# A sparse graph-attention layer on one core: the feed-forward pipeline one step shorter, its edges and gathers dealt by tables

## The chip, the cores and the metric

One core of one Trainium2 chip. The metric is device microseconds for one run of the whole kernel. TensorE is called PE here, VectorE DVE, ScalarE ACT, GpSimd POOL and SyncE SP.

## What is computed

One layer of multi-head attention over a sparse graph with 2048 nodes, 256 features and 8 heads, and a feed-forward part behind it:

```
hs = layer_norm(x) ; ht = layer_norm(h_target)
q = (ht @ Wq + bq) / sqrt(32) ; k = hs @ Wk + bk ; v = hs @ Wv + bv
probs = softmax over the sources s with adj[t, s] != 0 of q[t] . k[s], per head
ht = layer_norm(ht + (probs @ v) @ Wo + bo)
out = layer_norm(x + ht + gelu(ht @ W1) @ W2)
```

The adjacency matrix has about four edges in a row (each entry is set with a chance of 0.00195).

## The kernel before

Until about 90 us the kernel projects keys and values of all nodes to a scratch in DRAM, copies h_target and x side by side to another (`tab_scratch`, a row of 2 KB for each node, after which `rows_copied` stands at 32), and turns the adjacency matrix into lists of edges. The nodes are sorted by number of edges into 16 tiles of 128 targets. Tile m has 2, 2, 2, 3, 3, 3, 4, 4, 4, 5, 5, 5, 6, 7, 8 and 16 slots (m = 0 to 15): a slot is one neighbour of each of its 128 targets.

What follows, `finish(0)`, is what the change is about. For each tile it takes these things:

- POOL issues the gathers, one indirect DMA for each slot (`fetch(m, j)`, 79 of them, of key and value rows) and one for the tile's own rows (`fetch(m, -1)`). For tiles 0 and 1 (`DIRECT = 2`) the own rows come straight from h_target, and their rows of x later through `fetch_x`.
- DVE takes the statistics of the own rows (`take_stats`), POOL raises the variance to the power -0.5 (`rsqrt_group`, L772), DVE makes the shift (`make_shift`, L1741), ACT normalises, PE transposes (`turn_own`) and projects the query.
- DVE does the edges: `weigh_keys` (a product of keys with the query, L1599, a sum over each head, L1601, then the mask, the maximum and its subtraction), ACT the exponential, and `weigh_values` (`share`, a product L1640, sums L1646 to L1661, which leave the tile's context). Tiles of more than 5 slots are cut in pieces, 12a and 12b and so on. K3 is the key work of tile 3 here, V3 its value work.
- PE transposes the context (`turn_context`) and projects it onto the residual (`project_out`), which needs ACT's copy of the context. DVE takes the statistics of that, POOL the power, DVE the shift, ACT normalises (`normalise_res`), and PE transposes (`turn_h2`).
- PE does the feed-forward part in two halves, `mlp_in` (L984), gelu on ACT, `mlp_out` (L993), and adds the transposed residual (`add_h2`, L998). DVE adds x (`add_x`, L1676), and the same chain of statistics, power, shift and normalising leads to the row scatter by POOL (`save`, L778).

All this is software-pipelined by hand in steps s = -5 to 16, in which each engine runs its own fixed order. PE's step s holds the feed-forward part of tile s, `turn_context(s + 2)` (after the first half of `mlp_in` from step 2 on, so that the second half stands behind it), `turn_h2(s + 1)` and `project_out(s + 2)`. The edges are dealt to the steps from -3 on by an estimate of their work: half of a step's pieces before `add_x`, the others between `take_stats` and `make_shift`. The gathers are dealt by a rate (`RAMP_ROWS`, `STEP_ROWS`), half of them before the step's power on POOL and half behind it. POOL is one queue in order: a power stands behind the gathers issued before it. After the last gathers POOL drains once in each step.

The time shown ends with the last scatter. A path for dense graphs (`lo = TILES`) stands behind a flag and isn't run.

## Time and profile before

| | us |
|---|---|
| median of 3 runs (333.85 to 336.05) | 333.95 |
| the profiled execution | 333.58 |
| its span, first to last instruction | 331.8 |
| PE, DVE, ACT, POOL busy | 250.6, 223.1, 157.6, 186.1 |
| first gather issued | 90.53 |
| first `mlp_in` (step 0) | 133.30 |
| last gather issued | 261.72 |
| last context ready | 297.84 |

The span and what lies around it (1.78 us) make the profiled execution's time, which is 0.37 us under the median.

### The profile page before, as it was taken

The numbers are of one execution on the slowest core, as the hardware profiler recorded it, in microseconds if no ns is written. First come the engines' busy times: TensorE is split into PE (matmuls) and PEld (weight loads), VectorE is DVE, ScalarE is ACT, GpSimd is POOL, SyncE is SP. The second block draws the span as 40 slices with busy tenths as digits, with TensorE's granted clock in tenths as the row PEclk, the third lists the DMA queues.
The fourth block names the chain that finished last, engine by engine and source line by source line (L and its number), as shares of the span: only waits on it lengthen the run. The fifth ranks groups of instructions, "written<-read, shape, count | busy, mean of one in ns | idle before, by whom it ended". The sixth has DMA issues, their size and how long they took to land.

```text
span 331.8 us, 4310 instructions
## 1 busy us (share of the span) xinstructions
PE 250.6 (76%) x1383; PEld 195.3 (59%) x1383; DVE 223.1 (67%) x623; ACT 157.6 (47%) x282; POOL 186.1 (56%) x204
## 2 busy tenths in 40 slices
PE   6599895650216745979999899899895796949990
PEld 6344331210112524967999799789784695939980
DVE  3489879798825437367897698688885589780111
ACT  1656999610014323465767567746752244303220
POOL 8776522390077765725777888887878603111211
PEclk9789979875555565979999999999999599787996
DMA  6999999999546645424346564454565700000000
GB/s 159 401 396 418 418 391 328 355 303 333 207 131 185 191 132 169 143 64 126 113 147 171 159 174 144 132 166 147 161 174 168 155 28 16 18 0 16 16 17 24
DMA packets 23490, 58.04 MB, mean 175 GB/s; under 512 B 4051, under 2 KB 12517, under 8 KB 21414
## 3 DMA queue, kind: packets, MB, share of 16 engines
q0 software_dynamic: 8400, 27.01, 28.1%
q1 hardware_dynamic: 14228, 29.91, 24.7%
q10 hardware_dynamic: 834, 0.79, 1.1%
q8 instruction: 13, 0.21, 0.2%
q14 instruction: 15, 0.12, 0.1%
HBM read 51.40 MB, written 10.49 MB: 187 GB/s over the span
## 4 chain that ended last, share of the span: by engine, by line
PE 28%; POOL 26%; issue 17%; DVE 15%; ACT 9%; DMA 2%; another core or an unknown queue 1%; POOLq 0%; ACTq 0%; DVEq 0%
POOL arena L746 12%; PE score L984 8%; PE bank L993 7%; PE bank L854 4%; POOL rstd_late L772 4%; POOL tab L736 3%; DVE arena L1599 2%; DVE arena L1640 2%; DVE logits L1601 2%; POOL out_dram L778 2%; ACT arena L1174 2%; PE bank L962 2%; DVE arena L1646 2%; ACT query L1182 2%; ACT arena L1165 1%
## 5 line engine op out<-in xcount | busy, mean ns | idle before, releaser
L746 POOL DMA_INDIRECT arena<-kv_scratch,places x79 | 82.7, 1047 | 22.5 <-issue 22.5
L984 PE MATMUL score<-h_t,w_sb 128*128 128x128 f32 x512 | 66.3, 286 | 2.0 <-ACT h_t L1299 2.0
L984 PEld LDWEIGHTS score<-h_t,w_sb 128*128 128x128 f32 x512 | 64.9, 203 | 3.4 <-ACT h_t L1299 2.6
L993 PE MATMUL bank<-w_sb,gelu_t 128*128 128x256 f32 x256 | 62.1, 395 | 5.4 <-issue 4.8
L993 PEld LDWEIGHTS bank<-w_sb,gelu_t 128*128 128x128 f32 x256 | 50.3, 200 | 13.5 <-issue 5.4
L1245 ACT ACTIVATE gelu_t<-score 128x512 f32<-128x512 f32 x32 | 19.1, 597 | 68.2 <-PE score L984 51.2
L772 POOL TENSOR_TENSOR rstd_late<-var_late,minus_half 128x2 f32<-128x2 f32 (+2 forms) x22 | 22.2, 1009 | 34.6 <-DVE var_late L1711 24.3
L778 POOL DMA_INDIRECT out_dram<-y_out,places x16 | 17.1, 1071 | 34.0 <-ACT y_out L1291 30.8
L854 PE MATMUL bank<-tab,arena 128*128 128x512 f32 x64 | 32.9, 668 | 0.8 <-DVE arena L1423 0.4
L1599 DVE TENSOR_TENSOR arena<-arena,query 128x1024 f32<-128x1024 f32 (+3 forms) x22 | 24.6, 1116 | 7.9 <-ACT query L1276 6.5
L1676 DVE SCALAR_TENSOR_TENSOR y_sum<-bank,place_value,tab 128x256 f32<-128x256 f32 x16 | 7.7, 480 | 30.4 <-PE bank L998 29.2
L1640 DVE TENSOR_TENSOR arena<-arena,logits 128x1024 f32<-128x1024 f32 (+3 forms) x22 | 24.6, 1117 | 0.6
L1601 DVE TENSOR_REDUCE logits<-arena 128x32 f32<-128x1024 f32 (+3 forms) x22 | 24.4, 1111 | 0.8
L657 POOL TENSOR_TENSOR v_total<-v_total,arena 128x256 f32<-128x256 f32 x15 | 11.9, 796 | 22.4 <-DVE arena L1423 20.9
L854 PEld LDWEIGHTS bank<-tab,arena 128*128 128x128 f32 x64 | 13.4, 220 | 17.2 <-issue 16.3
L1252 ACT ACTIVATE tab<-tab,shift_late,rstd_late 128x256 f32<-128x256 f32 x16 | 9.4, 599 | 29.1 <-DVE shift_late L1741 29.1
L947 PE MATMUL score<-wq_sb,own_t 128*128 128x256 f32 x64 | 20.0, 443 | 0.0
L962 PE MATMUL bank<-wo_sb,ctx_t 128*128 128x256 f32 x64 | 19.0, 425 | 0.0
L1299 ACT ACTIVATE h_t<-bank,ln_col 128x128 f32<-128x128 f32 x32 | 12.9, 455 | 12.8 <-PE bank L971 10.0
L1646 DVE TENSOR_TENSOR arena<-arena 128x256 f32<-128x256 f32 (+1 forms) x32 | 17.1, 535 | 1.1
L736 POOL DMA_INDIRECT tab<-tab_scratch,places x14 | 15.2, 1088 | 4.0 <-issue 3.7
L1267 ACT ACTIVATE own_t<-score,ln_col 128x128 f32<-128x128 f32 x32 | 12.9, 456 | 8.1 <-PE score L937 7.9
(153 smaller groups left out, 447.2 us busy)
## 6 DMA issues: line engine op xcount, KB each, us to landing
arena<-in_adj_dram SPq DMA_DIRECT2D x6, 1024.0 KB, 11.8
w_sb<-in_adj_dram SPq DMA_DIRECT2D x6, 1024.0 KB, 12.9
kv_scratch<-arena SPq DMA_DIRECT2D x8, 512.0 KB, 9.7
tab<-in_x_dram SPq DMA_DIRECT2D x4, 512.0 KB, 11.0
own_t<-in_adj_dram SPq DMA_DIRECT2D x2, 1024.0 KB, 14.8
gelu_t<-in_adj_dram SPq DMA_DIRECT2D x2, 1024.0 KB, 11.4
tab_scratch<-in_L_gnn_h_target_dram SPq DMA_DIRECT2D x1, 2048.0 KB, 12.0
tab_scratch<-in_x_dram SPq DMA_DIRECT2D x1, 2048.0 KB, 16.5
```

The lines of the kernel that those rows point to most:

```text
L736: pool.indirect_dma_start(tab[:, m % TR, :], None, tab_dram[:, :], at).then_inc(own_gathered[m % OWN_RING], 16)
L746: pool.indirect_dma_start(kv_ring[:, ring_at[m] + j, :], None, kv_dram[:, :], at).then_inc(gathered[m][piece], 16)
L772: pool.tensor_tensor(rstd_late[:, a:b], var_late[:, a:b], minus_half[:, 0:b - a], ALU.pow).then_inc(rstd_late_ready, 1)
L778: pool.indirect_dma_start(out[:, :], bass.IndirectOffsetOnAxis(ap=places[:, at:at + 1], axis=0), y_out[:, n % YR, :], None).then_inc(y_sav ...
L854: mm = pe.matmul(proj_ps[i % 2], h_t[:, c % 2, k, i * P:(i + 1) * P], wkv[:, k, :], start=(k == 0), stop=(k == DK - 1))
L962: mm = pe.matmul(attn_ps[:, 0:D], ctx_t[:, n % 2, k, :], wo_sb[:, k, :], start=False, stop=(k == DK - 1), skip_group_check=True)
L984: mm = pe.matmul(hid_ps[(2 * n + half) % 3][:, f % 4 * P:(f % 4 + 1) * P], w1_sb[:, k, f * P:(f + 1) * P], h2_t[:, n % 2, k, :], start=(k ...
L993: pe.matmul(ff_ps[:, 0:D], gelu_t[:, n % 2, f, :], w2_sb[:, f, :], start=(f == 0), stop=False, skip_group_check=True)
L1599: dve.tensor_tensor(keys, keys, asked, ALU.mult).then_inc(score_step, 1)
L1601: dve.tensor_reduce(logits[:, r, a:b, :], keys.rearrange("p j (h d) -> p j h d", h=H), AX.X, ALU.add).then_inc(score_step, 1)
L1640: dve.tensor_tensor(by_head, by_head, part, ALU.mult).then_inc(weigh_step, 1)
L1646: dve.tensor_tensor(values[:, 0:half, :], values[:, 0:half, :], values[:, left - half:left, :], ALU.add).then_inc(weigh_step, 1)
```

## The change

- Steps -5 to -1 are gone for the sparse path. In their place every engine has a lead-in written out instruction by instruction: five tiles' own rows, K0 to K2, V0, V1, the first `project_out` and `turn_h2`, with a power for each row of statistics of its own (six, where steps -5 to -1 had five).
- In a step, `project_out(s + 1)` takes the place of `project_out(s + 2)`, right behind the first half of `mlp_in(s)`, and `turn_context(s + 2)` goes to the end of the step, behind `add_h2(s)`.
- `STEP_EDGES` says by name which pieces DVE does in each step behind `add_x`, between `take_stats` and `make_shift`, and behind `make_shift`. `OWN_STEP` says in which step a tile's own rows are taken, `OWN_AT` and `ROWS_BY` when gathers are issued.
- All own rows come from the copied table with their x: the two `fetch_x` go, and the first gather waits for `rows_copied`.
- ACT's order follows, and the two kinds of identity products (in `project_out` and `add_h2`) are written as transposes.

```diff
-    EDGES_LEAD = 3
-    RAMP = 0.35
-    DIRECT = 2
-    CONTEXT_LATE = 1
-    RAMP_ROWS, STEP_ROWS = 3, 6.5
+    OWN_STEP = [-5, -4, -3, -2, -1, 0, 1, 1, 2, 3, 4, 4, 5, 6, 7, 8]
+    OWN_AT = [0, 0, 3, 4, 10, 13, 18, 20, 29, 31, 39]
+    ROWS_BY = [(6, 12), (12, 16), (20, 23), (27, 30), (33, 37), (39, 45), (46, 50), (54, 58), (62, 67), (67, 71), (72, 76), (78, 81), ...
+    STEP_EDGES = [
+        ("V2 K3", "", "K4"),
+        ("", "V3", "K5 V4"),
+        ("V5", "", "K6"),
+        ("V6", "K7", "V7"),
+        ("", "K8", "V8"),
+        ("K9", "", "K10 V9"),
+        ("", "", "K11 K12a"),
+        ("V10", "K12b", "K13a V11"),
+        ("V12a", "V12b", "K13b"),
+        ("V13a", "K14a", "K14b"),
+        ("V13b", "K15a", "V14a"),
+        ("K15b", "", "V14b"),
+        ("K15c", "K15d", "V15a V15b"),
+        ("", "V15c", "V15d"),
...
+        lead_fetches = [(0, -1), (0, 0), (0, 1), (1, -1), (ROOT, 0), (2, -1), (1, 0), (ROOT, 1), (1, 1), (3, -1), (ROOT, 2),
+                        (2, 0), (2, 1), (4, -1), (ROOT, 3), (3, 0), (ROOT, "res"), (3, 1), (ROOT, 4), (3, 2)]
...
                 for k in range(DK):
                     pe.matmul(attn_ps[:, k * P:(k + 1) * P], own_t[:, own_of(n) % OWN_RING, k, :], ident[:, :], start=False,
-                              stop=False, skip_group_check=True)
+                              stop=False, is_transpose=True, skip_group_check=True)
...
@@ PE, finish @@
+                if lo == 0:
+                    for o in range(2):
+                        turn_own(o)
+                        project_query(o)
+                    turn_tally()
+                    turn_own(2)
+                    turn_context(0)
+                    project_out(0)
+                    project_query(2)
+                    turn_own(3)
+                    turn_h2(0)
+                    project_query(3)
...
+                for s in range(lo, hi):
+                    own_now = [own_of(lo + m) for m in own_work[s - lo - 1]]
+                    first = lo == 0 and s == 0
+                    mlp_in(s, 0)
+                    if s + 1 < hi and not first:
+                        project_out(s + 1)
+                    if own_now:
+                        turn_own(own_now[0])
+                    if first:
+                        turn_context(1)
+                    mlp_in(s, 1)
+                    if own_now:
+                        project_query(own_now[0])
+                    if first:
+                        project_out(1)
+                    mlp_out(s, 0)
+                    if len(own_now) > 1:
+                        turn_own(own_now[1])
+                    if s + 1 < hi:
+                        turn_h2(s + 1)
+                    mlp_out(s, 1)
+                    add_h2(s)
+                    if len(own_now) > 1:
+                        project_query(own_now[1])
+                    if lo == 0 and s + 2 < hi:
                         turn_context(s + 2)
@@ DVE @@
+            def lead():
+                def own_stats(m):
+                    take_stats(("lead", m), [m], None, None)
+
+                own_stats(0)
+                make_shift(("lead", 0))
+                own_stats(1)
+                make_shift(("lead", 1))
+                own_stats(2)
+                weigh_keys(0, 0, SLOTS[ORDER[0]])
+                make_shift(("lead", 2))
+                sum_tally()
+                weigh_values(0, 0, SLOTS[ORDER[0]])
+                own_stats(3)
+                weigh_keys(1, 0, SLOTS[ORDER[1]])
+                make_shift(("lead", 3))
+                take_stats(("lead", "res"), [], 0, None)
+                set_flag()
+                make_shift(("lead", "res"))
+                weigh_values(1, 0, SLOTS[ORDER[1]])
+                own_stats(4)
+                weigh_keys(2, 0, SLOTS[ORDER[2]])
+                make_shift(("lead", 4))
...
-                    early = 0 if s == lo - 1 else len(edges_now) if s < lo else len(edges_now) // 2
+                    first, second, rest = parts_of(s) if lo == 0 else ([], [], [])
                     key = (lo, s - lo)
-                    weigh_edges(edges_now[:early])
                     if s > lo:
                         add_x(s - 1)
+                    weigh_edges(first)
                     if key in group_at:
                         take_stats(key, [own_of(lo + m) for m in own_work[s - lo]],
                                    s + 1 if lo <= s + 1 < hi else None, s - 1 if s > lo else None)
-                    if s >= lo:
-                        weigh_edges(edges_now[early:])
+                    weigh_edges(second)
                     if key in group_at:
                         make_shift(key)
-                    if s < lo:
-                        weigh_edges(edges_now[early:])
+                    weigh_edges(rest)
```

## Rows read from the trace of the kernel before

**Rows 1.** The table by stage: busy of each engine, granted clock, DMA share, GB/s.

```profile
89.00:133.30 44.30, 22.15 (x71) 14.33 (x72) 21.13 (x75) 12.35 (x31) 30.79 (x34) 0.56 0.51 151
133.30:262.70 129.40, 117.04 (x764) 105.46 (x763) 99.37 (x230) 78.12 (x148) 97.26 (x89) 0.97 0.51 147
262.70:297.90 35.20, 27.48 (x171) 24.94 (x169) 27.62 (x56) 11.11 (x21) 7.35 (x6) 0.89 0.12 27
297.90:331.80 33.90, 25.37 (x155) 23.47 (x155) 4.71 (x18) 7.84 (x16) 5.99 (x7) 0.85 0.06 18
```

**Rows 2.** POOL's groups from 89 to 263 us: busy, mean ns, idle before.

```profile
L746 POOL DMA_INDIRECT arena<-kv_scratch,places x79 | 82.7, 1047 | 22.5 <-issue 22.5
L772 POOL TENSOR_TENSOR rstd_late<-var_late,minus_half 128x3 f32<-128x3 f32 (+2 forms) x16 | 16.4, 1025 | 11.1 <-DVE var_late L1711 9.7 <-issue 1.0
L778 POOL DMA_INDIRECT out_dram<-y_out,places x9 | 9.6, 1068 | 5.6 <-ACT y_out L1291 3.2 <-issue 2.4
```

**Rows 3.** The timeline of the last three steps and the end.

```profile
296.23 1.15 DVE L1646 TENSOR_TENSOR arena<-arena 128x512 f32<-128x512 f32 x2
297.41 0.42 DVE L1661 TENSOR_TENSOR context<-arena 128x256 f32<-128x256 f32 x1
298.37 3.62 PE L984 MATMUL score<-h_t,w_sb 128*128 128x128 f32 x16
301.79 3.96 PE L993 MATMUL bank<-w_sb,gelu_t 128*128 128x256 f32 x16
...
323.76 0.48 DVE L1676 SCALAR_TENSOR_TENSOR y_sum<-bank,place_value,tab 128x256 f32<-128x256 f32 x1 [5.98 <-PE bank L998]
```

**Rows 4.** The timeline of the lead-in, 90 to 134 us.

```profile
90.53 1.25 POOL L730 DMA_INDIRECT tab<-in_L_gnn_h_target_dram,places  x1 [14.99 <-DVE place_value L1568]
98.99 1.92 PE L947 MATMUL score<-wq_sb,own_t 128*128 128x256 f32 x4
110.26 0.95 POOL L736 DMA_INDIRECT tab<-tab_scratch,places  x1 [0.30 <-issue]
113.83 0.43 DVE L1697 BATCH_NORM_STATS2 stats_own<-tab 128x6 f32<-128x256 f32 x1 [2.81 <-DMA tab<-tab_scratch,places]
120.33 0.43 DVE L1697 BATCH_NORM_STATS2 stats_own<-tab 128x6 f32<-128x256 f32 x1 [4.66 <-DMA tab<-tab_scratch,places]
133.30 1.95 PE L984 MATMUL score<-h_t,w_sb 128*128 128x128 f32 x16
```

**Rows 5.** One step on PE in the steady part, from the timeline.

```profile
169.87 1.95 PE L984 MATMUL score<-h_t,w_sb 128*128 128x128 f32 x16
173.99 1.03 PE L947 MATMUL score<-wq_sb,own_t 128*128 128x256 f32 x4
174.85 3.62 PE L993 MATMUL bank<-w_sb,gelu_t 128*128 128x256 f32 x16
178.52 0.61 PE L998 MATMUL bank<-ident,h_t 128*128 128x128 f32 x4
180.39 1.95 PE L984 MATMUL score<-h_t,w_sb 128*128 128x128 f32 x16
```

**Rows 6.** Edge work on DVE by shape, from 93 to 298 us.

```profile
L1599 DVE TENSOR_TENSOR arena<-arena,query 128x1024 f32<-128x1024 f32 x10 | 12.2, 1224 | 0.0
L1646 DVE TENSOR_TENSOR arena<-arena 128x512 f32<-128x512 f32 x13 | 9.0, 692 | 0.4
```

**Rows 7.** Places of the timeline where something was late without a cause in the program.

```profile
162.88 1.22 DVE L1599 TENSOR_TENSOR arena<-arena,query 128x1024 f32<-128x1024 f32 x1
163.01 1.83 POOL L772 TENSOR_TENSOR rstd_late<-var_late,minus_half 128x3 f32<-128x3 f32 x1
174.58 0.90 POOL L772 TENSOR_TENSOR rstd_late<-var_late,minus_half 128x3 f32<-128x3 f32 x1
258.33 0.60 ACT L1245 ACTIVATE gelu_t<-score 128x512 f32<-128x512 f32 x1 [6.57 <-remote]
266.32 0.48 DVE L1676 SCALAR_TENSOR_TENSOR y_sum<-bank,place_value,tab 128x256 f32<-128x256 f32 x1 [4.53 <-PE bank L998]
```

More of the change, by code:

```diff
@@ L477, in graph_attention @@
[L477 to L491 removed]
+        LEAD_KEYS, LEAD_VALUES = 3, 2
@@ new lines, in stretch_of, with parts_of @@
+        def stretch_of(name):
+            m = int(name[1:].rstrip("abcd"))
+            letter = name[1:].lstrip("0123456789")
+            a, b = pieces_of(m)["abcd".index(letter) if letter else 0]
+            return KEYS if name[0] == "K" else VALUES, m, a, b
+        def parts_of(step):
+            return [[stretch_of(name) for name in part.split()] for part in STEP_EDGES[step]]
+        edge_work = {step: [w for part in parts_of(step) for w in part] for step in range(TILES + 1)}
+        for stage, first in ((KEYS, LEAD_KEYS), (VALUES, LEAD_VALUES)):
+            assert [w[1:] for some in edge_work.values() for w in some if w[0] == stage] == [
+                (m, a, b) for m in range(first, TILES) for a, b in pieces_of(m)]
@@ L508, in graph_attention @@
                     add_group(("own", o), [("own", o)])
-            for step in range(-LEAD, TILES + 1):
+            else:
+                for some in (0, 1, 2, 3, "res", 4):
+                    add_group(("lead", some), [("res", 0) if some == "res" else ("own", some)])
+            for step in range(0 if lo == 0 else -LEAD, TILES + 1):
                 some = [("own", own_of(lo + m)) for m in own_work[step]]
@@ L1003, in finish @@
                 hi = lo + TILES
-                for s in range(lo - LEAD, hi):
-                    own_now = [own_of(lo + m) for m in own_work[s - lo - 1]] if s > lo - LEAD else []
-                    if lo == 0 and s == 1 - EDGES_LEAD:
-                        turn_tally()
-                    if s >= lo:
-                        mlp_in(s, 0)
+                if lo == 0:
+                    for o in range(2):
[9 more added lines that the diff above has]
+                    project_query(3)
+                else:
+                    for m in range(LEAD - 1):
+                        turn_own(own_of(lo + m))
+                        project_query(own_of(lo + m))
+                    project_out(lo)
+                    turn_h2(lo)
@@ L1016, in finish @@
-                    for o in own_now[:1]:
-                        project_query(o)
-                    if s >= lo:
-                        mlp_out(s, 0)
-                    if lo == 0 and s <= CONTEXT_LATE and lo <= s + 2 < hi:
-                        turn_context(s + 2)
-                    if s >= lo:
-                        mlp_out(s, 1)
-                    if lo <= s + 1 < hi:
-                        turn_h2(s + 1)
-                    if s >= lo:
-                        add_h2(s)
@@ L1239, in exponential, with exponentials @@
                 act.activation(part, part, ACT.Exp).then_inc(exp_done, 1)
+            def exponentials(some):
+                for stage, m, _, b in some:
+                    if stage == KEYS and b == SLOTS[ORDER[m]]:
+                        exponential(m)
             def gelu(n, half):
```

184 lines of the change are left out of this document (79 added, 105 removed).

## Prediction

> **What bounds the kernel now.** I read the table by stage first, because the shares of the whole span hide that three engines take turns. Between 133.3 us (the first `mlp_in`) and 262.7 (the last gather issued) PE is busy 117.0 of 129.4 us, DVE 99.4 and POOL 97.3 [rows 1]. The second view, POOL's groups, shows that POOL is nearly full there all the same: each of the 79 gathers has 22.5/79 = 0.28 us of "issue" in front, so one costs 1.05 + 0.28 = 1.33 us, a save (9.6 + 2.4)/9 = 1.33, a power 1.03 and about 0.2 behind it [rows 2]. After 262.7 no gather is left, and the work that ends last is DVE's: pieces b to d of K15, then V14 and V15, until the last context at 297.41 + 0.42 = 297.8 [rows 3]. Then PE does the second half of tile 13's feed-forward part and all of tiles 14 and 15 in its fixed order, `add_x` starts at 323.76, and the span ends at 331.8. The kernel from 90.5 us on is therefore three stretches in a row, and I forecast each: the lead-in (90.5 to 133.3), steps 0 to 13 (133.3 to 297.8, 164.5 us), the tail (34.0 us).
>
> **The lead-in.** Both versions do K0 to K2, V0, V1 and the first `project_out` before step 0. In the old one a step's statistics wait for own rows far ahead: DVE stands 2.81 us for tile 5's row, gathered from 110.26 and used at 113.83, and 4.66 us for the next at 120.33, and the first residual's chain stands behind them [rows 4]. The written-out order asks only for tiles 0 to 4. I follow it:
> - Gather of row 0 at 90.5 as before. The new wait for `rows_copied` costs nothing if the copy has landed; POOL went past the same wait at tile 2's row before. A row of 2 KB takes 113.83 - 110.26 = 3.6 us from issue to use [rows 4], about 0.4 more than the 1 KB rows that go.
> - Query 0 is projected at 98.99 as before, queries 1 and 2 follow in about 4.6 and 7 us, because `turn_own` waits until the query before is copied and PE runs at its lower level there (mean granted clock 0.56 from 89 to 133.3 [rows 1]; four products take 1.92 us against 1.03 later [rows 4, 5]). `project_out(0)` ends near 110.5, its statistics, power and shift near 112. POOL stands idle about 2.6 us at this power and 1.3 at the next: a new loss, as gathers are queued behind.
> - `project_query(2)`, `turn_own(3)`, normalising, `turn_h2(0)` and `project_query(3)` follow one another on PE: the first `mlp_in` starts near 118.3. That is 15.0 us before 133.3.
> - DVE ends K2 at 116.7 and waits for tile 2's exponential (behind ACT's long list) until 119.6, 13.7 us before its old start of step 0. POOL ends its 14 lead gathers at 116.3. It had issued about 19 by then, so it is some 6 us behind its old place.
>
> **Steps 0 to 13.** The pieces in them are the same as before (V2 and K3 up to V15), and so are the statistics. DVE's busy time for them is 99.4 + 27.6 = 127.0 us in 286 instructions [rows 1]; an instruction starts a little behind its predecessor's end (0.03 us between the first two rows of [rows 3]; I take 0.05 as the mean, an estimate, since small ones in chains wait longer), so they occupy about 143 us, and 164.5 - 143 = 21.5 were waits. Part of the waits had no cause in the program: ACT stood 6.57 us before the gelu at 258.33, and DVE 4.53 for PE behind it [rows 7].
> Added is a loop within one step. `project_out(s + 1)` now ends about 3.0 us into PE's step (half an `mlp_in` 1.8, bias, two transposes and four products 1.2), and `turn_h2(s + 1)` stands about 8.1 us into it [rows 5] (half an `mlp_in` 1.8 us, a query 1.0, `mlp_out` 3.5, by the distances between starts). Between them lie DVE's statistics (0.9), the pieces in the middle column, the wait for POOL, a power (0.9), shift (0.2) and ACT (0.6). In front there are the pieces of the first column. A 4-slot piece costs 2 x 1.22 us for keys and 1.22 + 0.69 + 0.43 for values, with some 0.6 to 0.9 more for a tile's end [rows 6]. Steps 3 and 7 hold over 6 us in the first two columns: PE waits some 2 and 4.5 us there, elsewhere 0 to 3. PE can afford it: a step with a query took 180.39 - 169.87 = 10.5 us [rows 5], and 14 steps of at most that are 147, under DVE's 143 plus waits. The transposes halve four instructions' worth in `add_h2` and `project_out`, 0.4 us a step, on PE alone; nothing of it reaches the end but 1 us in the tail.
> POOL: step 0 has 12 gathers, six before its power (116.3 + 8 = 124.5), but the power waits for `project_out(1)` until about 128.5: 4 us idle. From there the hand walk goes: DVE starts `add_x` of steps 4, 8 and 12 at 169, 219 and 261 us. DVE waits at `make_shift` in steps 0, 2, 3, 5 and 6 because gathers stand before the power (1 to 3 us each), 3.6 in step 0 for PE, about 1 us for an exponential in four steps. The last gather is issued near 260, 81 x 1.33 + 11 x 1.33 + 12 x 1.2 = 137 us of work and 7 of idle behind 116.3. It lands 3.6 later, in time for K15d at 264.6. V15d ends at 284.0. That is 143 of work and 21.4 of waits from 119.6, so the same length as before: 164.4. It holds no unexplained standstill, and the old stretch had about 5 us of them on DVE's path. I add 3 for such: 287.0.
>
> **A rule on the power.** A power on three values took 0.90 us at 174.58, but 1.83 at 163.01, where DVE's product of two arrays in SBUF ran from 162.88 for 1.22 us [rows 7]. The Trainium skill (SBUF — State Buffer, Who interferes with whom) says that a `tensor_tensor` with both inputs in SBUF and a GpSimd operation that reads SBUF exclude each other for a whole instruction. The trace agrees at these two rows. By the rule alone the new order would be a little better: it has a product beside the power in 9 steps of 14 (those with a middle column), the old one in all 14, and 5 x 0.93 us less would give 309. I keep the mean of 1.03, because in the five others DVE has nothing to do but wait for the power.
>
> **The tail.** Now `turn_context(15)` ends step 13 and doesn't stand before its second half. Gone from behind the last context are half an `mlp_in` and an `mlp_out`, 3.62 + 3.96 with overlap 7.2 us at that clock, `turn_h2` and `add_h2`, 0.7, and 1 us of slow clock and transposes [rows 3, 5]. 34.0 - 9.0 = 25.0 us: turn and copy 0.4, step 14 with `project_out(15)` 8.7, step 15 7.9, then 331.8 - 323.76 = 8.0. This holds if PE is through step 13 when V15d ends; by the walk it is just behind (283.8).
>
> **Sum.** 287.0 + 25.0 = 312.0 us of span, plus 333.58 - 331.8 = 1.8: 313.8, or 314, against 333.58 for the profiled execution and 333.95 for the median (which I leave as the same). It is 13.7 by the lead, 9.0 by the tail and -3 by the allowance, since the walk's 164.4 replaces 164.5 that held standstills already.
>
> **Rivals.**
> 1. POOL gives the lead's gain back. POOL is 6 us behind at 116 and idle 8 us by 128.5; any further idle puts the last gather past 270, and K15d with V15 takes 20 us behind it. For: the old last gather was at 262 and the new one is at 260 in my walk, without slack. Then DVE ends near 297 as before and only the tail is won: 333.6 - 9.0 = 324.6.
> 2. The tables fill DVE's waits. Each piece is placed by name, and DVE may wait 9 us where it waited 21. Against: the powers stand behind gathers in order. 119.6 + 143 + 9 + 25.0 + 1.8 = 298.4.
> 3. Slower: the loop of one step. PE, DVE and POOL meet twice in a step (at the power, at `turn_h2`), with one step of slack less. If each step has one gather more before its power (1.33) and a power held by a product (0.93 more [rows 7]), it costs 2.26 us x 14 = 31.6 on the walk: 345. The point where it decides is (333.6 - 313.8)/14 = 1.4 us a step. Against: PE had 12 us to spare in the long stretch [rows 1].
> 4. The change shifts nothing that counts: the lead's gain lost in the steps as in 1, and PE not through step 13 at V15, so that the tail's gain goes too: 333.
>
> **How the numbers follow.** Forecast 0.50 (306 to 321), rival 1 0.22, rival 2 0.17, rival 3 0.06, rival 4 0.05. Within 1% (3.3 us) is about what a measurement of this kernel tells from no change. The range goes from 300 to 327, which leaves out the best part of rival 2, and rivals 3 and 4. Faster by over 1%: 0.89; within 1%: 0.06; slower: 0.05.
>
> **What would show it.** In the changed kernel: the first `mlp_in` near 118 and DVE's V2 near 120; the last gather near 260; the last context near 287; no `mlp_in` of tile 13 behind it; 25 us from there to the end; PE idle before `turn_h2` by waits for ACT in several steps, above all step 7. I am wrong if PE's first `mlp_in` is later than 125, if POOL idles over 15 us before its last gather, or if DVE's stretch from V2 to V15 is over 175 or under 158 us.

## The result and the profile after

The changed kernel took 317.38 us (median of 4 runs, 317.19 to 318.49), the kernel before 333.9 on the same occasion (332.99 to 336.05): ratio 0.950, 95% interval 0.946 to 0.954, faster. I had said 314 and 300 to 327. The profiled execution took 318.49, with a span of 316.8. Executions over 1.5% above the fastest of the same kernel are left out of every ratio here; three of four were such in experiments 2 and 5, which have no ratio, and the traces of experiments 2, 5 and 8 are of such executions.

The table by stage of the changed kernel, cut where mine were cut: start of step 0, last gather issued, last context. The columns are those of [rows 1].

```profile
89.00:115.10 26.10, 13.79 (x44) 8.30 (x44) 14.89 (x55) 8.47 (x21) 17.26 (x20) 0.56 0.46 131
115.10:266.40 151.30, 128.68 (x824) 114.54 (x824) 113.51 (x271) 94.12 (x171) 115.90 (x103) 0.97 0.52 148
266.40:291.80 25.40, 19.11 (x112) 16.75 (x111) 20.00 (x38) 9.40 (x17) 5.47 (x5) 0.89 0.14 36
291.80:316.80 25.00, 17.98 (x118) 16.32 (x116) 4.71 (x17) 5.59 (x11) 5.97 (x7) 0.91 0.07 24
```

The first row took 44.3 us and now takes 26.1. The last took 33.9 and takes 25.0. What lies between is 176.7 us (151.3 + 25.4) in place of 164.6. So some 27 us were won at the two ends and 12 are longer in the middle (part of that is DVE work that has only moved there from the lead-in, as said below). The middle is what the experiments are about.

The lead-in, from the timeline (it answers to [rows 4]):

```profile
90.50 1.25 POOL L739 DMA_INDIRECT tab<-tab_scratch,places  x1 [15.00 <-DVE place_value L1611]
98.94 1.92 PE L946 MATMUL score<-wq_sb,own_t 128*128 128x256 f32 x4
...
109.53 1.91 PE L946 MATMUL score<-wq_sb,own_t 128*128 128x256 f32 x4
114.17 1.03 PE L946 MATMUL score<-wq_sb,own_t 128*128 128x256 f32 x4
115.12 2.05 PE L983 MATMUL score<-h_t,w_sb 128*128 128x128 f32 x16
```

The first own row and the first query stand where they stood. The last query of the lead takes 1.03 us where the others take 1.91: the granted clock is 0.50 from 108 to 112 us and 1.00 from 112.2 on, so PE is at the higher of its two levels (2.4 GHz) again before step 0.

POOL's groups from 89 to 268 us, against [rows 2]:

```profile
L749 POOL DMA_INDIRECT arena<-kv_scratch,places x79 | 88.0, 1114 | 22.2 <-issue 22.2
L769 POOL TENSOR_TENSOR rstd_late<-var_late,minus_half 128x1 f32<-128x1 f32 (+3 forms) x18 | 17.8, 991 | 13.2 <-DVE var_late L1752 12.0 <-issue 0.9
...
L775 POOL DMA_INDIRECT out_dram<-y_out,places x10 | 12.0, 1197 | 3.0 <-issue 3.0
```

The same 79 gathers take 88.0 us in place of 82.7. The issue gap in front of each is unchanged.

The end, from the timeline, against [rows 3]:

```profile
291.36 0.42 DVE L1704 TENSOR_TENSOR context<-arena 128x256 f32<-128x256 f32 x1
...
293.70 1.95 PE L983 MATMUL score<-h_t,w_sb 128*128 128x128 f32 x16
...
309.81 0.48 DVE L1717 SCALAR_TENSOR_TENSOR y_sum<-bank,place_value,tab 128x256 f32<-128x256 f32 x1 [4.17 <-PE bank L997]
```

From the last context's end (291.78) to `add_x` of tile 15 are 18.0 us; they were 25.9.

Three things in this trace were not in my working. One is a stall on POOL, between its last save before step 13 and the power of step 13:

```profile
278.06 1.11 POOL L775 DMA_INDIRECT out_dram<-y_out,places  x1 [7.29 <-ACT y_out L1306]
288.10 0.72 POOL L769 TENSOR_TENSOR rstd_late<-var_late,minus_half 128x2 f32<-128x2 f32 x1 [8.93 <-issue]
```

POOL waits for nothing that the profile shows, for 8.93 us. The program has a `pool.drain()` at this place, in both kernels. In the old one the same 8.93 us ended at 273.31 and DVE had edge work meanwhile; here DVE and PE wait for the power.

The second follows from it. My tail asked that PE be through step 13 when the last context is ready (291.78). It wasn't:

```profile
289.66 0.69 PE L970 MATMUL bank<-ident,h 128*128 128x128 f32 x2 [3.08 <-ACT h L1298]
290.14 3.29 PE L992 MATMUL bank<-w_sb,gelu_t 128*128 128x256 f32 x8
...
293.49 0.38 PE L928 MATMUL bank<-ident,context 128*128 128x128 f32 x2
```

PE had stood 3.08 us for the `h` of tile 14, and came to `turn_context(15)` 1.7 us after the context.

The third is that PE's results come late although its own rows run on:

```profile
166.96 1.95 PE L983 MATMUL score<-h_t,w_sb 128*128 128x128 f32 x16
...
172.00 0.60 ACT L1260 ACTIVATE gelu_t<-score 128x512 f32<-128x512 f32 x1 [2.62 <-remote]
173.45 0.43 DVE L1746 BATCH_NORM_STATS2 stats_late<-bank 128x6 f32<-128x256 f32 x1 [4.88 <-remote]
```

`mlp_in` should be through at 168.9, and gelu starts at 172.00. "Remote" is the profile's word for a wait whose releaser it can't name; the old trace had such places too [rows 7]. I call them standstills. The name says no more than that: no run here shows what PE, or the record of it, does in them. From 100 to 300 us, ACT and DVE together spent 18.8 us in such waits here, and 21.2 in the old trace. The waits of the two engines overlap.

### The profile page after: what moved, and what is told of

It is laid out like the page before. It is cut to its first block, busy times and chain, and to the rows that moved or that the text cites. A ratio compares the mean times of both kernels' runs of the same rounds, so it can differ in the third digit from the quotient of the medians.

```text
span 316.8 us, 4181 instructions
## 1 busy us (share of the span) xinstructions
PE 236.4 (75%) x1316; PEld 183.1 (58%) x1319; DVE 223.7 (71%) x625; ACT 165.7 (52%) x286; POOL 189.4 (60%) x203
## 3 DMA queue, kind: packets, MB, share of 16 engines
q1 hardware_dynamic: 14228, 29.91, 25.9%
## 4 chain that ended last, share of the span: by engine, by line
PE 32%; POOL 21%; issue 13%; DVE 10%; ACT 10%; DMA 8%; another core or an unknown queue 4%; SPq 1%; POOLq 0%; ACTq 0%; DVEq 0%
POOL arena L749 12%; PE bank L992 8%; PE score L983 7%; DMA tab_scratch<-in_x_dram 5%; PE bank L853 4%; POOL rstd_late L769 3%; PE bank L961 3%; PE score L946 3%; POOL tab L739 3%; POOL out_dram L775 2%; ACT arena L1188 2%; ACT query L1196 2%; DMA arena<-kv_scratch,places 2%; ACT arena L1179 2%
## 5 line engine op out<-in xcount | busy, mean ns | idle before, releaser
L749 POOL DMA_INDIRECT arena<-kv_scratch,places x79 | 88.0, 1114 | 22.2 <-issue 22.2
L992 PE MATMUL bank<-w_sb,gelu_t 128*128 128x256 f32 x256 | 66.5, 408 | 0.0
L983 PE MATMUL score<-h_t,w_sb 128*128 128x128 f32 x512 | 62.5, 276 | 0.0
L983 PEld LDWEIGHTS score<-h_t,w_sb 128*128 128x128 f32 x512 | 60.3, 193 | 0.6 <-ACT h_t L1314 0.3
L992 PEld LDWEIGHTS bank<-w_sb,gelu_t 128*128 128x128 f32 x256 | 51.5, 208 | 7.1
L769 POOL TENSOR_TENSOR rstd_late<-var_late,minus_half 128x1 f32<-128x1 f32 (+3 forms) x23 | 21.1, 918 | 31.7 <-DVE var_late L1752 21.6
L1260 ACT ACTIVATE gelu_t<-score 128x512 f32<-128x512 f32 x32 | 19.1, 597 | 30.7 <-PE score L983 22.9
L853 PE MATMUL bank<-tab,arena 128*128 128x512 f32 x64 | 31.1, 636 | 1.3 <-DVE arena L1466 1.1
L739 POOL DMA_INDIRECT tab<-tab_scratch,places x16 | 17.3, 1079 | 19.3 <-DVE place_value L1611 15.0
L970 PE MATMUL bank<-ident,h 128*128 128x128 f32 x32 | 7.8, 331 | 25.0 <-ACT h L1298 21.3
L970 PEld LDWEIGHTS bank<-ident,h 128*128 128x128 f32 x32 | 3.7, 153 | 30.0 <-ACT h L1298 25.2
L1746 DVE BATCH_NORM_STATS2 stats_late<-bank 128x6 f32<-128x256 f32 x16 | 6.9, 429 | 18.3 <-PE bank L961 10.1
L946 PE MATMUL score<-wq_sb,own_t 128*128 128x256 f32 x64 | 19.1, 427 | 0.0
L1282 ACT ACTIVATE own_t<-score,ln_col 128x128 f32<-128x128 f32 x32 | 12.9, 454 | 11.4 <-PE score L936 5.3
L1314 ACT ACTIVATE h_t<-bank,ln_col 128x128 f32<-128x128 f32 x32 | 12.9, 453 | 10.2 <-PE bank L970 9.5
## 6 DMA issues: line engine op xcount, KB each, us to landing
arena<-in_adj_dram SPq DMA_DIRECT2D x6, 1024.0 KB, 12.2
tab<-in_x_dram SPq DMA_DIRECT2D x4, 512.0 KB, 11.6
tab_scratch<-in_L_gnn_h_target_dram SPq DMA_DIRECT2D x1, 2048.0 KB, 12.1
```

The costliest lines, as they stand in the source:

```text
L739: pool.indirect_dma_start(tab[:, m % TR, :], None, tab_dram[:, :], at).then_inc(own_gathered[m % OWN_RING], 16)
L749: pool.indirect_dma_start(kv_ring[:, ring_at[m] + j, :], None, kv_dram[:, :], at).then_inc(gathered[m][piece], 16)
L769: pool.tensor_tensor(rstd_late[:, a:b], var_late[:, a:b], minus_half[:, 0:b - a], ALU.pow).then_inc(rstd_late_ready, 1)
L853: mm = pe.matmul(proj_ps[i % 2], h_t[:, c % 2, k, i * P:(i + 1) * P], wkv[:, k, :], start=(k == 0), stop=(k == DK - 1))
L946: mm = pe.matmul(own_ps[:, D:KV], own_t[:, o % OWN_RING, k, :], wq_sb[:, k, :], start=False, stop=(k == DK - 1))
L983: mm = pe.matmul(hid_ps[(2 * n + half) % 3][:, f % 4 * P:(f % 4 + 1) * P], w1_sb[:, k, f * P:(f + 1) * P], h2_t[:, n % 2, k, :], start=(k ...
```

## The experiments

All are edits of the changed kernel. They ran on four occasions, and the kernel before ran beside them each time: 331.7 us on the first (four kernels), 335.3 on the second (four), 328.8 on the third (three), 328.9 on the fourth (one). Differences are taken within an occasion wherever I can. In the record the first and the fourth occasion have the same chip number (13); the second has 6 and the third 11. Before experiment 12 I compared traces with the changed kernel's first one, which has standstills; where experiment 12's trace, which has none, changes a reading, it is said there.

**1. `turn_context` back in mid-step (the tail).** From step 2 it stands again before the second half of `mlp_in`, not at the end of PE's step.

```
+                    if lo == 0 and s > 1 and s + 2 < hi:
+                        turn_context(s + 2)
...
-                    if lo == 0 and s + 2 < hi:
+                    if lo == 0 and s <= 1:
                         turn_context(s + 2)
```

> The changed kernel with turn_context(s + 2) put back in front of the second half of mlp_in(s), from step 2 on (ACT's copy of it again behind the second gelu). Tail theory: 7 us of feed-forward work of tile 13 stand behind the last context again, so the last context comes at the same 291.8 us and the tail is 32 to 34 us instead of 25.0: 325 us. Rival (PE is not through step 13 anyway when the last context is ready, so the order hardly matters): within 2 us of 317.4.

322.75 us (319.04 to 323.41), ratio 0.973 (0.965 to 0.981). PE's waits from 116 to 300 us:

```profile
PE bank L970 <- ACT h L1300: 19.1, 11, 3.9
PE bank L928 <- DVE context L1708: 10.7, 1, 10.7
```

PE stands 10.7 us at `turn_context` for the last context, with half an `mlp_in` and an `mlp_out` of tile 13 behind it. The last context ends at 289.6 and the span at 320.7: a tail of 31.1 us in place of 25.0. So 6.1 of the 9 us that the tail won are this one move.

**2. PE's old order, two tiles ahead (the loop in one step).** `project_out(1)` is done in the lead, and `project_out(s + 2)` at the end of PE's step. `turn_context(s + 2)` is back in mid-step as in experiment 1.

```
+                    turn_context(1)
+                    project_out(1)
...
-                    if s + 1 < hi and not first:
-                        project_out(s + 1)
...
+                    if s + 2 < hi:
+                        project_out(s + 2)
```

> The changed kernel with PE's old order: project_out(s + 2) at the end of step s, turn_context(s + 2) in the middle of it, and project_out(1) in the lead-in; tables and lead-in stay otherwise. Theory of the loop in one step: PE stood 25 us in front of turn_h2, DVE 15 us in front of make_shift; with a step of slack PE's waits there fall under 10 us and the stretch from V2 to V15 shrinks from 175 us by 5 to 10; the tail is 8 us longer and the lead-in 2: about 320 us. Rival (POOL's gathers in order set the stretch, whatever the order on PE): it stays at 173 to 177 us, and the whole is 327 us.

326.33 us (318.09 to 329.08, the 318.09 without a trace); last context at 292.7, tail 32. PE's wait for ACT's `h` at `turn_h2` is 21.0 us in 10 places; it is 20.0 in 9 in the changed kernel from 116 to 300 us. With a whole step of slack given back, PE waits as long. The stretch from V2's first row (117.40) to the last context is 175.3 us, to the tenth what it is in the changed kernel's first profile (with 12.2 us of waits without a releaser for 18.8 there). So the loop within one step does not set its length, as far as one trace tells. I read it so that `h` is late because the power is late: DVE waits 15.8 us for powers here (12.1 there).

**3. Eight gathers fewer (POOL's queue).**

```
+        LEFT_OUT = [(m, SLOTS[ORDER[m]] - 1) for m in range(6, 14)]
...
-                else:
+                elif (m, j) not in LEFT_OUT:
                     if (m, j) == (0, 0):
...
```

> The changed kernel with the last gather of each of the tiles 6 to 13 left out (8 of 79; the slot's old content is used, so those edges are wrong), DVE's work unchanged. It is 8 x 1.35 = 11 us less for POOL. If POOL's queue sets the stretch from V2 to V15, it shrinks by 7 to 11 us: 307 to 310 us. If DVE's own work and its meetings with PE set it: under 3 us: 315 to 317. There are 103 indirect DMAs in it in place of 111: by the count theory of the 8.93 us that standstill is gone, by the drain theory it is there.

306.26 us (305.03 to 307.68), ratio 0.926 (0.919 to 0.932).

```profile
L750 POOL DMA_INDIRECT arena<-kv_scratch,places x71 | 76.6, 1079 | 19.8 <-issue 19.8
```

POOL is spared 11.4 + 2.4 = 13.8 us and the last context ends at 278.0, 13.8 before its place in the changed kernel's first profile. About 1.7 of that was there already at the first context, and this profile has fewer standstills (3.6 us in place of 18.8), so 13.8 is more than the gathers' worth. Against experiment 12, which has no standstill, it is much less: the stretch from V2 to the last context is 164.0 us here and 167.2 there, 3.2 shorter for 15.6 us less of gathers on POOL. (This profile has one standstill, of 3.6 us, so without it at most 6.8.) With eight gathers fewer POOL is no longer full: from 116 us to its last gather it waits 11.6 us for DVE and ACT. DVE had the same work and followed POOL's queue only in part. The stall before the power was still there, 8.27 us.

**4. Nothing ahead of the power in the queue, from step 2 to step 11.** The gathers that the table puts in front of a step's power go behind it.

```
-    ROWS_BY = [(6, 12), (12, 16), (20, 23), (27, 30), (33, 37), ...
+    ROWS_BY = [(6, 12), (12, 16), (16, 23), (23, 30), (30, 37), ...
```

> The changed kernel with no gather in front of the power in steps 2 to 11 (all of a step's gathers behind it). Theory of the loop in one step (DVE's 15 us and PE's 25 us of waits are the gathers in front of powers): these waits fall by half and the whole by 3 to 6 us: 312 to 314. Queue theory: POOL itself stands idle until each step's statistics are there, 1 to 3 us a step more, the last gather comes later than 268 by 5 to 15 us, and the whole takes 320 to 330.

329.38 us (328.37 to 332.7), ratio 0.984 (0.981 to 0.986), 9 us slower than experiment 7 on the same occasion. Its profile has 31.8 us of waits without a releaser and that of experiment 7 has 20.2, so how much of the 9 is the queue's is not shown.

```profile
L769 POOL TENSOR_TENSOR rstd_late<-var_late,minus_half 128x1 f32<-128x1 f32 (+3 forms) x23 | 22.5, 979 | 45.0 <-DVE var_late L1752 34.5
```

POOL stands 34.5 us for the variances (21.6 in the changed kernel) with its gathers behind the waiting power. The last gather is issued at 281.06 in place of 266.42. Where gathers stand in front of the power, the power is late; where they stand behind it, the gathers are.

**5. The powers of the steps on DVE** (two Newton rounds there, none of these powers on POOL).

```
-            return key[0] != "own"
+            return key[0] in ("lead", TILES)
...
```

> The changed kernel with the power of each of the steps 0 to 16 worked out on DVE (a first guess from the exponent and two rounds of Newton, 7 small instructions, 1.3 us) in place of POOL's. POOL has 17 x 1.2 = 20 us less to do and no power stands behind its gathers; DVE doesn't wait for POOL at make_shift (15 us), but has 14 x 1.3 = 18 us more of its own. Queue theory (POOL's queue in order sets the stretch from V2 to V15): the last gather comes 10 to 14 us earlier, the stretch shrinks by 5 to 10, and the tail by 0 to 2: 308 to 313 us. Rival (DVE's own work is the bound as much as POOL): 317 or more.

355.14 us (349.16 to 355.96). DVE's busy time goes from 223.7 to 242.8, so the added work is 19 us and the loss nearer 35. The profile has 60 us of waits without a releaser on ACT and DVE; the first `add_x` is already 7.6 us late. How much of the loss is theirs can't be read off. This experiment decides nothing about the queue: the 19 us on DVE are one cause, and the rest is open.

**6. The port that DVE and POOL share: one-input sums in place of the edge products.**

```
-                dve.tensor_tensor(keys, keys, asked, ALU.mult).then_inc(score_step, 1)
+                dve.tensor_reduce(spare[:, a:b, :], keys.rearrange("p j (h d) -> p j h d", h=H), AX.X,
+                                  ALU.add).then_inc(score_step, 1)
```

(and the same for the product with the weights.)

> The changed kernel with the two products of the edges (keys with the query, values with the weights: two arrays from SBUF) replaced by sums over the same elements (one array from SBUF) into a spare tile, so that scores and contexts are wrong and DVE's time is nearly the same (1.11 us each in both forms). In the changed kernel gathers that start within a product take 1.9 to 2.3 us in place of 0.95, and all 79 take 88.0 us. Lock theory (a gather's issue on POOL waits until DVE's product of two SBUF arrays is over): the long ones go, the 79 take under 80 us, the last gather is issued 6 to 9 us earlier, and with it the whole ends near 309. Rival (gathers are long because of their own data or DMA): they stay at 1.11 us in the mean, and the whole at 317.

322.73 us (322.42 to 326.66), ratio 0.968 (0.960 to 0.975): so the time didn't come down to the 309 that I expected, but POOL's durations did what they should:

```profile
L750 POOL DMA_INDIRECT arena<-kv_scratch,places x79 | 77.5, 981 | 22.2 <-issue 22.2
...
L770 POOL TENSOR_TENSOR rstd_late<-var_late,minus_half 128x1 f32<-128x1 f32 (+3 forms) x23 | 17.0, 738 | 43.6 <-DVE var_late L1754 34.5
```

Gathers are 10.5 us cheaper and powers 4.1, and POOL spends it waiting. On ACT and DVE there are 35.6 us of waits without a releaser. No run has this kernel without them; experiments 10 and 11 make the same comparison with half the bytes, and there they are absent.

**7. PE's products without `is_transpose`.**

```
-                              stop=False, is_transpose=True, skip_group_check=True)
+                              stop=False, skip_group_check=True)
```

> The changed kernel with the identity products of project_out and add_h2 as plain matrix products again (twice as many instructions). Prediction: 0.4 us a step on PE, of which only about 1 us in the tail counts: 318 to 319 us, tail 26 us. Rival (PE is in the loop of each step, so each step pays): 14 x 0.4 = 6 us, 323 us.

320.35 us (319.43 to 325.92), ratio 0.957 (0.954 to 0.960). The last context is at 291.6 (291.8 in the changed kernel), the tail 26.0 in place of 25.0: by one trace of each the cheaper form is worth about 1 us, in the tail.

**8. No drain.**

```
-                        pool.drain()
```

> The changed kernel without POOL's drains behind the last gather. In both kernels POOL stood 8.93 us in front of one power after the gathers were over. If a drain causes it, it goes, DVE doesn't wait 2.1 us at make_shift(13) nor PE 3.1 us at turn_h2(14), and the kernel takes 314 to 315.5 us. Rival (it comes with the 107th indirect DMA, since 107 were issued before it in both kernels): the 8.93 us stay where they are, 317 us.

317.35 us (314.97 to 321.04), ratio 0.957 (0.947 to 0.967).

```profile
283.47 1.62 POOL L769 TENSOR_TENSOR rstd_late<-var_late,minus_half 128x2 f32<-128x2 f32 x1 [4.86 <-DVE var_late L1752]
...
308.57 1.03 POOL L775 DMA_INDIRECT out_dram<-y_out,places  x1 [1.11 <-ACT y_out L1306]
```

The power no longer waits: it starts at 283.47, and the last scatter is out at 309.6 in place of 314.0. But the span ends at 319.3, 9.7 us behind that scatter, where the changed kernel ends 2.8 behind its own and every other profile here 2.7 to 4.0. In this execution the time that was removed stands at the end. Two of the four runs took 315; they have no trace, so whether they escaped it is not known. As a whole the interval (0.947 to 0.967) holds the changed kernel's 0.950: no gain is shown.

**9. The drain in a gap.** It goes in front of the save of step 12, where POOL had 7.29 us of idle time.

```
+                    if lo == 0 and step == FIRST_DRAIN:
+                        pool.drain()
                     if s > lo:
                         save(s - 1)
...
```

> Whole computation kept. POOL's first drain is moved from behind the save of step 12 (where it stood 8.93 us until 288.10 and DVE and PE waited for the power behind it) to in front of that save, where POOL had 7.29 us of idle time (270.77 to 278.06). Theory (the 8.93 us are the time of a drain after many indirect DMAs, and must be paid once, wherever it stands): the drain lasts from about 270.8 to 279.7, the save is 1.6 us later, which nobody waits for; the power of step 13 comes near 283.5 as in the kernel without the drain, last context near 289.0 (before 291.8), and the end, without the late cost that the kernel without the drain had in some runs, near 314.5 (313.5 to 315.5). Rival (the drain waits for the last gathers or saves to finish in some other way, and stands just as long at any later place, or makes the following drains long): a second stall of several us before a later power, 317 to 318. Rival (the save held back by 2 us makes ACT or POOL late in step 13): 316 to 317.

303.62 us (301.96 to 305.4, 6 runs), ratio 0.924 (0.920 to 0.928): 11 us better than the 314.5 I expected, and I expected only 4 of it from this edit.

```profile
267.86 1.23 POOL L776 DMA_INDIRECT out_dram<-y_out,places  x1 [9.53 <-issue]
270.79 1.61 POOL L770 TENSOR_TENSOR rstd_late<-var_late,minus_half 128x2 f32<-128x2 f32 x1 [1.70 <-DVE var_late L1755]
```

The stall is 9.53 us, in front of a save that nobody waits for, and the power behind it waits 1.70 us for its variance alone. But step 11 had ended at 253.48 already, 12 us early, with the program unchanged up to there. The trace has not one wait without a releaser. Whether that is the edit's doing is what run 12 asks.

**10. Half the bytes per gather.**

```
-                    pool.indirect_dma_start(kv_ring[:, ring_at[m] + j, :], None, kv_dram[:, :], at).then_inc(
+                    pool.indirect_dma_start(kv_ring[:, ring_at[m] + j, 0:D], None, kv_half[:, :], at).then_inc(
...
```

> All 79 edge gathers of the steps and the lead bring 1 KB of each of 128 rows in place of 2 KB (from a view of half rows), and the value products use the keys' half, so scores and contexts are other numbers; the count of gathers, their places in POOL's order and every instruction of the engines stay. What it is to tell: what the standstills are in which PE's results come 2 to 5 us late and the trace names no releaser (in the changed kernel 8.1 us of DVE's waits, 10.7 of ACT's between 116 and 300 us). Theory T (DMA traffic: the standstills fall in stretches in which the 16 DMA engines are 70% busy or more with gathered rows): the DMA share falls to about 0.4 there, waits without a releaser fall under 3 us on each of the two engines, POOL's own rate stays (1.1 us a gather and 0.28), and the time falls by what of the standstills lay on POOL's or DVE's path: 310 to 315. Rival P (they come from POOL's issuing of descriptors back to back, whatever the bytes): waits without a releaser stay at 6 us or more on DVE or ACT, 316 to 318.5. Rival N (gathers themselves get faster with fewer bytes): the mean of a gather falls under 1.0 us, 305 to 310.

310.56 us (309.02 to 313.33), ratio 0.943 (0.937 to 0.948). No standstill, but run 9, with all the bytes, had none either, so it says nothing of their cause. It does say that bytes don't set a gather's price on POOL (with 2 KB a row it is 1136 ns in experiment 12):

```profile
L750 POOL DMA_INDIRECT arena<-kv_scratch,places x79 | 91.4, 1157 | 22.2 <-issue 22.2
```

**11. Half the bytes and one-input sums.** The edits of experiments 6 and 10 together.

> As the kernel with half the bytes per gather, and besides DVE's two edge products of every piece are replaced by sums with one input (as in the earlier run, which had gathers of 981 ns on the mean but 322.7 us in all, more than the changed kernel); scores and contexts are other numbers. Theory T (gathers closer together in time filled the DMA engines and made more standstills, which ate what POOL had saved): with half the bytes the standstills are gone, gathers keep about 0.98 us, and the time comes out where the rule on the shared port alone put it, 306 to 311, below the kernel with half the bytes by 3 us or more. Rival P (standstills come with POOL's rate of issue, not with bytes): 319 to 324 again. Rival M (the sums themselves are slower for DVE or order the work worse): no standstills, but 316 to 321, with DVE's or ACT's named waits longer.

299.33 us (299.19 to 299.69), ratio 0.910 (0.906 to 0.914).

```profile
L751 POOL DMA_INDIRECT arena<-kv_scratch,places x79 | 77.8, 985 | 22.2 <-issue 22.2
```

11.2 us below run 10, whose only difference is the form of DVE's products. DVE is busy as long in both (222.5 and 223.3 us), so it isn't the sums that are cheaper. In the traces the stretch from V2 to the last context is 158.1 us against 168.4, 10.2 shorter, for 13.6 us less of gathers and 1.5 of powers. POOL has room again: from 116 us to its last gather it waits 9.5 us for DVE and ACT.

**12. The changed kernel again, unaltered.**

> The changed kernel itself, unaltered, on another occasion. The last batch ran where the kernel before took 328.75 us, and none of its three profiles had a standstill without a releaser; the one with the earlier drain took 303.6 us, far under my 314.5. Theory V (the standstills belong to the chip or the occasion, not to the program: without them the changed kernel takes about 308, and the earlier drain is worth 4 to 5 us of it): if no standstill shows in this profile, 306 to 310, with the step ends of the kernel with the earlier drain up to step 11 (first at 125.4, the twelfth at 253.5, within 3 us), then the 8.9 us before the power of step 13. If standstills show (8 us or more on ACT or DVE), 315 to 319 again and the twelfth step end past 262. Rival W (placing the drain earlier changed the whole run, by code alignment or otherwise): no standstill here and yet 314 or more, or standstills here on an occasion where the kernel before takes 329 or less.

308.14 us (305.6 to 310.2, 6 runs) against 328.9: ratio 0.934 (0.930 to 0.937), with no wait without a releaser in the profile, as theory V had it. This occasion's chip number is that of experiments 1, 2, 3 and 8, which had standstills, so they are no fixed property of one chip. The ends of steps 3, 4 and 11 (`add_x`), first in the changed kernel's first profile, then in this one:

```profile
167.11 0.48 DVE L1717 SCALAR_TENSOR_TENSOR y_sum<-bank,place_value,tab 128x256 f32<-128x256 f32 x1
180.77 0.48 DVE L1717 SCALAR_TENSOR_TENSOR y_sum<-bank,place_value,tab 128x256 f32<-128x256 f32 x1
...
265.91 0.48 DVE L1717 SCALAR_TENSOR_TENSOR y_sum<-bank,place_value,tab 128x256 f32<-128x256 f32 x1 [0.30 <-PE bank L997]
```

```profile
163.35 0.48 DVE L1717 SCALAR_TENSOR_TENSOR y_sum<-bank,place_value,tab 128x256 f32<-128x256 f32 x1
174.57 0.48 DVE L1717 SCALAR_TENSOR_TENSOR y_sum<-bank,place_value,tab 128x256 f32<-128x256 f32 x1
...
256.58 0.48 DVE L1717 SCALAR_TENSOR_TENSOR y_sum<-bank,place_value,tab 128x256 f32<-128x256 f32 x1 [0.30 <-PE bank L997]
```

V2 starts 1.17 us apart in the two (116.48 and 115.31). At the end of step 3 they are 3.8 apart, of step 4 6.2, then level to step 7, 8.0 at step 8 and 9.3 at steps 10 and 11. Each growth sits where the first profile has a standstill (gelu or statistics at 134.06, 161.32, 172.00, 227.00 and 249.20) and nowhere else. The standstills cost the first run 9.3 - 1.2 = 8.1 us.

This trace also shows the middle without them. The stretch from V2's first row to the last context, and POOL's waits for the input of a power, from 116 us to its last gather at 257.08:

```profile
115.31:282.52 167.21, 144.60 (x924) 128.95 (x924) 132.88 (x304) 102.97 (x184) 119.74 (x108) 0.97 0.49 139
```

```profile
POOL rstd_late L769 <- DVE var_late L1752: 1.5, 2, 1.2
```

With another 0.3 us before an own row, POOL waits 1.8 us for another engine in 141 us, against 8.0 in the first profile. It is full: what puts the last gather where it is are its own entries.

Against run 12, the earlier drain of run 9 is worth 308.14 - 303.62 = 4.5 us. By the traces, from `add_x` of step 11 to the end of the span, it is 51.5 us there and 46.7 in run 9, so 4.8: 3.1 of them before the last context and 1.7 in the tail (23.9 in place of 25.6). The two kernels ran on different occasions and chips, but the kernel before took the same beside both (328.75 and 328.9). The intervals of the two ratios (0.930 to 0.937, 0.920 to 0.928) don't touch. This version beats both kernels.

## Why the prediction was right

- **The sum.** 313.8 against 318.49 for the profiled execution and 317.38 for the median. Two errors of size are in it, which cancel in part: the lead 3.1 us too late, and the steps 7.9 too short. So the three stretches and their gains were right, and the closeness of the sum is in part luck. By one sign that I had named I was wrong: the stretch from V2 to V15 was 175.3 us, over my 175.
- **The lead-in** was won as said, and more: step 0's `mlp_in` at 115.12 (I had 118.3), V2 at 116.48 (119.6). `project_out(0)` ended at 109.5 (I had 110.5) and its shift at 111.2 (112). The other 2 us came behind it: I went on with the lower level's durations, and the granted clock was 1.00 from 112.2; that this makes all of the rest is not shown. The own row took 3.69 us from issue to use, as said.
- **Steps 0 to 13.** I had 167.4 from V2 to the last context, 3 of them an allowance for standstills; measured 175.3. Run 12 has 167.2 (115.31 to 282.52), so the total was right where no standstill fell, but by luck. I wrote that the pieces in the steps are the same as before, V2 and K3 up to V15. They are not: in the old trace the products of K3 and V2 stand ahead of 133.3,

```profile
126.50 0.96 DVE L1599 TENSOR_TENSOR arena<-arena,query 128x768 f32<-128x768 f32 x1 [0.28 <-issue]
...
132.43 0.69 DVE L1640 TENSOR_TENSOR arena<-arena,logits 128x512 f32<-128x512 f32 x1
```

  and so do the statistics of three more own rows. DVE's work in the new stretch is 132.9 us in 304 instructions, where I took the old 127.0 in 286, which is 6 us too little. (127.0 + 286 x 0.05 is also 141.3 and not the 143 that I wrote.) The stall at the drain (3.1 us of it before the last context) was missing too, and so was the higher price of the gathers. Against these stand the allowance of 3, which nothing used, and waits that were shorter than my 21.4: with my own 0.05 us an instruction, 148.1 us are work and 19.1 waits. In the first profile, where standstills fell, the allowance should have been 8.1. The old kernel's 21.2 us of such waits were in its trace; I had looked at two of them [rows 7].
- **Gathers.** I priced one at 1.05 + 0.28 us from [rows 2]. In the new order it was 1.11 + 0.28 (1.14 in run 12). The last was issued at 266.42, not near 260, with 88.0 us of gathers for 82.7 and 8.0 us of waits. In run 12 it is 257.08: 89.8 us of gathers, but 1.8 us of waits where my walk had 7.
- **The rule on the shared port** I applied to the powers alone. It holds for the gathers, at this place among others:

```profile
150.09 1.23 DVE L1642 TENSOR_TENSOR arena<-arena,query 128x1024 f32<-128x1024 f32 x1
150.17 2.03 POOL L749 DMA_INDIRECT arena<-kv_scratch,places  x1 [0.20 <-issue]
```

  The shortest gather takes 0.94 us, and this one 2.03. Of the 21 gathers of this trace that start inside such a product, 20 end 0.8 to 0.9 us behind the product's end, a little less than an undisturbed gather's time. Runs 10 and 11 price it: without two-input products, 13.6 us less for the gathers and 11.2 us less in time. The Trainium skill (SBUF — State Buffer, Who interferes with whom) has the exclusion for operations of GpSimd that read SBUF, and infers that preparing descriptors is not stalled by a `tensor_tensor`. These gathers are held by a `tensor_tensor`, and the measurement decides. They also read their row numbers (`places`) from SBUF, so the exclusion for reads may be all that holds them; no run here tells that read and the preparing of descriptors apart.
- **The loop in one step** (rival 3) was not there: run 2 gives the step back, and the stretch and PE's waits stay. The sign that I had named did come, without being a cost: PE's longest wait for `h` is 4.27 us, in step 7.
- **POOL gives the lead's gain back** (rival 1, 324.6). Its mechanism is real: in run 12 POOL is full up to its last gather, and run 11 shortens the stretch by relieving it. It is near another limit, though: run 3 takes 15.6 us off POOL against run 12 and wins 3.2 of them, run 11 takes 15.1 off against run 10 and wins 10.2, and in both POOL then waits for the others. Run 4 points the same way, but with more standstills. The lead's gain was not lost: without standstills the stretch from V2 on was 167.2 us, about what I had, because POOL waited 1.8 us where my walk had it idle for 7.
- **The tables fill DVE's waits** (rival 2, 298.4) did not happen: on the quiet occasion DVE still waits 20.1 us at `make_shift`, in 13 places.
- **The tail** was 25.0 us, as summed, and run 1 shows 6.1 of its 9.0 us of gain to be the move of `turn_context`; about 1 is the transposes, and the rest is not split. The hit is in part luck: my condition, PE through step 13 at the last context, failed by 1.7 us. From the context to the last `add_x` were 18.0 us, where I had 17.0, and behind it 7.0 where I had 8.0. What I missed is that the drain was uncovered: 4.5 us by the times of runs 9 and 12, and only 1.7 of it in the tail.
- **Transposes**: about 1 us in the tail, as said (run 7).

## What to carry to other kernels

Where two engines take turns and a third feeds both from one queue, read the price of that queue's entries with the other engines' work beside them: here a new order of the same gathers made each 6% dearer. Look also whether that queue is full before you count what it would save: eight gathers fewer were worth 3 of 15.6 us, since another limit lay close behind. A fixed cost such as a drain belongs where its engine is idle and nobody waits, and when a change takes cover away, look for what it had covered. When a result is off by some per cent, run the kernel itself a second time before explaining the difference: here that moved it by 9 us, twice what the best edit gave.

## What was unexpected of the hardware

- A drain on POOL behind some 100 indirect DMAs takes 8.93 us (8.27 with eight fewer; 9.53 in the earlier place). Left out, 6.9 us more stood between the last scatter and the end, in the one traced execution.
- A gather of 128 rows costs POOL 0.94 to 0.98 us alone, with 1 KB or 2 KB a row (0.98 in both runs with one-input sums), and longer where it starts inside a DVE product of two arrays in SBUF: by the rest of that product, up to 2.31 us in all (21 such gathers in the changed kernel's first profile, 0.96 to 2.31 us).
- Standstills of up to 9.2 us in which PE's results are late and the profile names nobody: in all ten profiles of the first three sessions of runs (the old kernel, the first result, experiments 1 to 8), from 3.6 to 60 us of waits, and in none of the last four. On PE's side the granted clock is 1.00 around them at 166 to 174 us. They cost the changed kernel 8 us and probably the old one about 5, by its medians (333.9 and 328.9), so a ratio taken with them (0.950) and without (0.934) differs by more than either interval. The three profiles with the most (32 to 60 us) are edits of POOL's order or load, but all three ran on one occasion, beside one with 20. The changed kernel had them on one occasion and not on another. What they are stays open.
